# The first two FFN chunks prepared inside the attention, the weight units loaded earlier, and the experts chosen one softmax sooner

## The chip, the core and the metric

The kernel runs on one core of one Trainium2 chip. The metric is the device time of one execution in microseconds (us). The engines named below are TensorE (PE, its weight loads PEld), VectorE (DVE), ScalarE (ACT), GpSimd (POOL) and the SyncE queue (SP), which issues every DMA of this kernel.

## What is computed

The input has 4 images of 256 channels and 48 x 48 pixels. A block of attention by convolution is followed by a mixture of experts:

```
xn = layernorm over channels of x
k  = relu(conv7x7 with dilation 2 (xn, w1) + b1)          # 256 -> 128 channels
a  = softmax(relu(batchnorm(conv1x1(k, w2) + b2)))        # 49 maps
x  = x + sum over the 49 taps of shifted(xn) * a[tap]
t  = tokens of x;  n = layernorm(t)
g  = softmax(mean over tokens of n @ Wr + br)             # one row of 8 gates per image
g  = softmax(g * min(1, capacity / load))                 # capped gates
e  = the 2 largest of g; w = softmax of the two
y  = sum over the two experts of w * (gelu(n @ W1[e] + b1[e]) @ W2[e] + b2[e])
t  = t + layernorm(y + n) * gamma + beta
```

## The kernel before

Because of the dilation of 2, every 48 x 48 image is kept as four images of 24 x 24 pixels (by the parity of row and column). So there are 16 such images (`IMGS`), four to a batch `b` (`B` = 4). The numbers are float16 pairs: a high half and the low rest, so that each product takes three matmuls.

The program has two phases, each a block of its own; the second starts when every engine has ended the first.

**First phase (`mix_phase`), convolution.** For each batch the convolution runs over 14 points `k` (`NP`), with two halves of the channels (`c`) of 21 matmuls each (line 1316). A batch also does, between the points, what the batch before it still needs. In the last batch (b = 3) PE does after point k the logits of image k of batch 2 (`logits`, lines 1353 and 1357), and in the middle of point k the turning of the attention map of image k - 2 (line 1373). `logits` of one image waits until DVE has run `shift_logits` of the image before (line 1015 to 1020), since they share a PSUM bank. From point 9 on PE spreads the taps of the first 12 images (line 1404) in three PSUM banks; the fourth item waits until DVE has taken the low half of the first (`spread_low`, line 1129).

DVE runs its part of the same loop: for point k the layernorm's own work, `shift_logits` and `normalise` of image k - 1, the low half of the map, and `take_unit` (line 1098): the largest magnitude of one of 17 units of expert weights (8 of W1, one of all b1, 8 of W2), 512 KB each but for the small one. The dictionary `UNITS_SLOT` says how many units DVE takes at the end of each point. The units are loaded by SP (line 673) into three stages (`STAGES`) that lie in the dead tile `xs`; the load of unit u waits for `take_unit(u - 3)`. SP works strictly in the order of its program; before the change the first unit stands behind the layernorm numbers (lines 652 to 663), the attention maps (line 657, 2 x 459 KB) and the table `spread` (line 665, 684 KB).

**First phase, attention.** For each of the 16 images n, PE sums the taps (`attend`, line 1420, 39 matmuls in three groups, three PSUM banks), ACT adds the residual out of PSUM (`evict`, line 840), DVE takes the token statistics (`statistics`, lines 1063 to 1071) and sums of tokens (`accumulate`, line 1093), POOL raises to the power -0.5 (line 726), and SP stores the tokens and, for every fourth image, their statistics (`t_scratch`, `stat_scratch`, lines 642, 647, 649). The tables of the first 12 images (`EARLY`) lie in the first half of the tile `V`, `V[:, 0]`, which is dead once image 11 is attended. `load_back` brings the normalised images from DRAM.

**Second phase (`ffn_phase`).** The 9216 tokens are 24 chunks of 384, six to a batch. Of a chunk SP loads the tokens and their two statistics (lines 1666 and 1668), ACT normalises them (line 1837) and takes the high halves (line 1807), DVE takes the low halves (line 1916), and SP turns them by a transposing DMA into `xT` (line 1676). PE then runs layer 1 (line 2131, 48 matmuls) and layer 2 (line 2145, 72 matmuls). At the start, DVE, PE and ACT compute the gates in a chain of short instructions (lines 1882 to 1951). SP waits for the indices of the two experts, reads them, and loads their W1, b1, W2 and b2 (lines 1696 to 1709). ACT and DVE split W1 into halves (lines 1790 and 1959). For chunk 0 layer 1 waits for the turned tokens and for the high half of the first expert's W1.

## Time and profile before

| what | us |
|---|---|
| median of 3 runs | 980.85 |
| lowest and highest | 979.34, 983.98 |
| the profiled execution, its own time | 980.27 |
| its span in the trace | 978.5 |
| PE busy | 909.7 (93% of the span) |
| DVE busy | 699.5 (71%) |
| ACT busy | 528.8 (54%) |
| POOL busy | 141.8 (14%) |

The trace's clock starts at the span's start. The first phase ends at 576.2 us. The first phase's last batch of convolution begins near 345 us, its attention at 465 us. PE is the busiest engine; an interval in which PE is idle, or runs at the lower granted clock, is what to look for. "Granted clock" is the share of the full TensorE clock in a stretch; its two levels are 1.2 and 2.4 GHz (0.5 and 1.0). A row of a timeline gives start, duration, engine, line, operation, output and inputs, the number of instructions merged in it, and in square brackets the idle time ahead and what ended it.

### The profile page before, as it was taken

Reading aid. Unit: us, or ns where it says so; the run is one execution under the profiler, and the core shown is the slowest. Engines: PE = TensorE matmul, PEld = TensorE weight load, DVE = VectorE, ACT = ScalarE, POOL = GpSimd, SP = SyncE. Lnnn points to the kernel's source line nnn. Section 1 sums busy time; section 2 is a strip of 40 time slices with the busy share of each in tenths; the row PEclk is TensorE's granted clock in tenths of the full one; section 3 lists DMA queues with packets and bytes.
Section 4 is the critical chain, followed back from the end, with each engine's and each line's share of the span. In section 5 each row is a group of like instructions: output and inputs, shape, how many; then the busy total and the mean of one; then the engine's idle time right before and its main releaser. Section 6 shows DMA issues by size and latency. Waiting matters only on the chain. (4 is left out here: it accounts for less than half of the span.)

```text
span 978.5 us, 19546 instructions
## 1 busy us (share of the span) xinstructions
PE 909.7 (93%) x7659; PEld 755.1 (77%) x7659; DVE 699.5 (71%) x1824; ACT 528.8 (54%) x981; POOL 141.8 (14%) x164
## 2 busy tenths in 40 slices
PE   3787999999999969999999947999999999999997
PEld 2776888888888858888999934777777777777776
DVE  3797567477658619836579866878877887788777
ACT  4796343434444211133445438686867777687851
POOL 1100110000010200200113220111221212112122
PEclk9999999999999998989999968999999999999999
DMA  9721311132200144720558446354255335424211
GB/s 215 217 61 52 95 49 50 50 91 62 63 26 25 45 138 131 200 50 2 132 150 220 133 121 164 90 128 96 64 152 110 66 85 159 98 50 98 66 33 49
DMA packets 134826, 95.01 MB, mean 97 GB/s; under 512 B 63579, under 2 KB 129516, under 8 KB 134636
## 3 DMA queue, kind: packets, MB, share of 16 engines
q1 hardware_dynamic: 134734, 93.77, 37.5%
q8 instruction: 60, 0.98, 0.4%
q14 instruction: 32, 0.26, 0.1%
HBM read 54.91 MB, written 29.40 MB: 86 GB/s over the span
## 5 line engine op out<-in xcount | busy, mean ns | idle before, releaser
L1316 PE MATMUL pM<-V,U 128*128 128x264 f16 (+3 forms) x2352 | 294.6, 283 | 0.0
L1316 PEld LDWEIGHTS pM<-V,U 128*128 128x128 f16 x2352 | 230.5, 99 | 44.6
L1824 ACT ACTIVATE gf<-pH,b1c,sc 128x384 f32<-128x384 f32 x192 | 127.7, 669 | 83.8 <-issue 67.2
L2131 PE MATMUL pH<-xT,w1h 128*128 128x384 f16 x768 | 157.9, 329 | 5.8 <-DMA xT<-xs 3.4
L2145 PE MATMUL pY<-w2h,gh 128*128 128x256 f16 x576 | 157.0, 273 | 0.3 <-DVE w2l L1989 0.3
L2145 PE MATMUL pY<-w2h,gl 128*128 128x256 f16 x576 | 157.0, 273 | 0.0
L2145 PE MATMUL pY<-w2l,gh 128*128 128x256 f16 x576 | 157.0, 273 | 0.0
L1997 DVE SCALAR_TENSOR_TENSOR gl<-gf,sc,gh 128x384 f16<-128x384 f32 x192 | 112.1, 620 | 50.2 <-ACT gh L1815 50.2
L2131 PEld LDWEIGHTS pH<-xT,w1h 128*128 128x128 f16 x768 | 75.0, 99 | 55.6 <-ACT gf L1824 4.8
L1815 ACT ACTIVATE gh<-gf,sc 128x384 f16<-128x384 f32 x192 | 115.4, 616 | 0.0
L775 ACT CAST V<-pV 128x336 f16<-128x336 f32 x96 | 42.0, 437 | 133.3 <-PE pV L1287 133.3
L941 DVE TENSOR_TENSOR V<-pV,V 128x336 f16<-128x336 f32 x96 | 47.7, 501 | 71.3 <-ACT V L775 71.1
L2131 PE MATMUL pH<-xT,w1l 128*128 128x384 f16 x384 | 94.5, 328 | 0.0
L1757 POOL TENSOR_TENSOR tb<-tk,bet 128x768 f32<-128x768 f32 x24 | 43.6, 1817 | 302.1 <-DVE z L2009 278.7
L1287 PE MATMUL pV<-Td,xs 96*128 96x168 f16 x576 | 58.3, 237 | 5.7 <-DVE xs L1056 5.7
L2145 PEld LDWEIGHTS pY<-w2h,gh 128*128 128x128 f16 x576 | 56.4, 98 | 8.3 <-issue 0.7
L2145 PEld LDWEIGHTS pY<-w2l,gh 128*128 128x128 f16 x576 | 56.4, 98 | 7.6
L2145 PEld LDWEIGHTS pY<-w2h,gl 128*128 128x128 f16 x576 | 56.4, 98 | 6.5
L702 POOL TENSOR_TENSOR rstd<-ve,mhalf 96x6 f32<-96x6 f32 x16 | 21.2, 1322 | 258.3 <-DVE nmean L936 258.3
L2131 PEld LDWEIGHTS pH<-xT,w1l 128*128 128x128 f16 x384 | 37.8, 98 | 25.2 <-issue 0.7
L1287 PEld LDWEIGHTS pV<-Td,xs 96*128 96x128 f16 x576 | 46.7, 99 | 10.5 <-issue 6.4
L758 ACT ACTIVATE xa<-xa,shift,rstd 96x256 f32<-96x256 f32 x96 | 49.9, 594 | 7.6 <-POOL shift L704 7.5
(252 smaller groups left out, 1357.2 us busy)
## 6 DMA issues: line engine op xcount, KB each, us to landing
xa<-in_xt SPq DMA_DIRECT2D x16, 576.0 KB, 6.4
xs_scratch<-xs SPq DMA_DIRECT2D x16, 576.0 KB, 4.3
tk<-t_scratch SPq DMA_DIRECT2D x24, 384.0 KB, 3.8
out<-o SPq DMA_DIRECT2D x23, 384.0 KB, 2.9
xs<-in_ew SPq DMA_DIRECT2D x16, 512.0 KB, 4.3
U<-xs_scratch SPq DMA_DIRECT2D x16, 480.0 KB, 4.7
V<-in_w1g SPq DMA_DIRECT2D x6, 784.0 KB, 8.4
w1r<-in_ew SPq DMA_DIRECT2D x8, 512.0 KB, 4.3
```

Of the source, the lines that this page charges most:

```text
L702: nc.gpsimd.tensor_tensor(rstd[:, n % 2], ve[:, n % 2], mhalf[:, :], ALU.pow).then_inc(rstd_step, 1)
L758: last = nc.scalar.activation(xa[:, n % XBUFS, t, :], xa[:, n % XBUFS, t, :], ACT.Identity, bias=shift[:, n % 2, t:t + 1], scale=rstd[:, n ...
L775: nc.scalar.copy(v_out(0, m), v_in(m)).then_inc(vhi_ready, 1)
L941: tt(v_out(1, m), v_in(m), v_out(0, m), ALU.subtract).then_inc(vlo_ready, 1)
L1287: last = nc.tensor.matmul(v_in(m)[:, :, r * TR * TILES:(r + 1) * TR * TILES], xs[:, n % 2, 2 * g + r, a, c * P:(c + 1) * P], Td[:, d, :], ...
L1316: return nc.tensor.matmul(out[:, :, first:end], U[:, k, hi_u, piece, :], V[:, b % 2, hi_v, k, c, :, first + TILES * d:end + TILES * d], st ...
L1757: nc.gpsimd.tensor_tensor(tb[:, s], tk[:, m % TBUFS], bet[:, None, :].broadcast_to([P, CT, C]), ALU.add).then_inc(bias_added, 1)
L1815: nc.scalar.activation(gh[:, s, j, :], gf[:, (JB * m + j) % GBUFS, :], ACT.Copy, scale=scale_of(G_UP)).then_inc(gh_ready, 1)
L1824: nc.scalar.activation(gf[:, (JB * m + j) % GBUFS, :], pH[:, (JB * m + j) % HBUFS, 0:CN], ACT.Gelu, bias=b1c[:, j // FB, j % FB:j % FB + 1 ...
L1997: stt(gl[:, sl, j, :], gf[:, (JB * m + j) % GBUFS, :], scale_of(G_UP), gh[:, sl, j, :], ALU.mult, ALU.subtract).then_inc(g_step, 1)
L2131: last = nc.tensor.matmul(pH[:, (JB * m + j) % HBUFS, 0:CN], w[:, k, c, f * P:(f + 1) * P], xT[:, s, x, c, :], start=(i == 0), stop=(i == ...
L2145: last = nc.tensor.matmul(pY[:, t, 0:C], g[:, s, j, t * P:(t + 1) * P], w[:, j // FB, j % FB, :], start=(i == 0), stop=(i == len(terms) - 1))
```

## The change

Four things are changed.

1. The tile `V` and the buffers of the FFN's tokens (`tk`, `tnk`, `xs`, `xs2`, `xT`, in a new class `Tokens`) share one place: the latter are views of `V`. Those that chunks 0 and 1 need lie in `V[:, 0]`.
2. In the attention, SP loads chunks 0 and 1 after image 11 (`CHUNKS_AT`); ACT normalises and splits them after `evict(12)` and `evict(13)`; DVE takes the low halves at the end of its work for images 13 and 14; SP turns them after it has stored images 13 and 14. The same steps are gone from the start of the second phase.
3. The loads of the first three weight units stand ahead of the layernorm numbers, the maps and `spread`. `take_unit` is spread differently over the points: none at k = 0, one at k = 1, two at k = 2 to 6, three at k = 7 and 8 (before: one at k = 0 and two at each of k = 1 to 8).
4. The experts' indices are found from the capped gates ahead of the second softmax, which keeps their order. `MAX` and `MAX_INDEX` run there; `MAX` runs once more after it. SP waits for step 11 in place of 16.

```diff
-STAGES, UNITS_SLOT = 3, {0: 1, 1: 2, 2: 2, 3: 2, 4: 2, 5: 2, 6: 2, 7: 2, 8: 2}
+STAGES, UNITS_SLOT = 3, {1: 1, 2: 2, 3: 2, 4: 2, 5: 2, 6: 2, 7: 3, 8: 3}
...
+            sp.wait_ge(v_turned, V_TURNS * IMGS)
+            for s in range(2):
+                sp.wait_ge(xs_stored[s], 16 * IMGS // 2)
+            load_units(range(STAGES))
             sp.wait_ge(ln_taken, 2)
...
             sp.dma_start(G[:, :, :], spread_d).then_inc(g_loaded, 16)
-            for s in range(2):
-                sp.wait_ge(xs_stored[s], 16 * IMGS // 2)
-            sp.wait_ge(v_turned, V_TURNS * IMGS)
-            for u in range(UNITS):
...
+            load_units(range(STAGES, UNITS))
...
                 if n in STATS_AT:
                     store_stats(STATS_AT[n])
+                if n == CHUNKS_AT:
+                    sp.wait_ge(o_ready, T_SUMS * EARLY)
+                    sp.wait_ge(stats_stored[0], 32)
+                    for m in range(EARLY_CHUNKS):
+                        sp.wait_ge(t_stored[m], 32)
+                    for m in range(EARLY_CHUNKS):
+                        tokens.load(sp, 0, m)
+                if n - CHUNKS_AT - 2 in range(EARLY_CHUNKS):
+                    tokens.turn(sp, 0, n - CHUNKS_AT - 2)
...
+                if n - CHUNKS_AT - 1 in range(EARLY_CHUNKS):
+                    tokens.normalise(act, 0, n - CHUNKS_AT - 1)
+                    tokens.take_high(act, 0, n - CHUNKS_AT - 1)
...
+                if n - CHUNKS_AT - 2 in range(EARLY_CHUNKS):
+                    tokens.take_low(dve, 0, n - CHUNKS_AT - 2)
...
-            for m in range(2):
-                load_chunk(0, m)
-            sp.wait_ge(r_step, 16)
+            load_chunk(0, EARLY_CHUNKS)
+            sp.wait_ge(r_step, IDX_STEP)
             load_experts(0)
...
             do(tt(r[:, 6, :], r[:, 5, :], r[:, 4, :], ALU.mult))
+            do(nc.vector.max(r[:, 0, :], r[:, 6, :]))
+            do(nc.vector.max_index(idx[:, :], r[:, 0, :], r[:, 6, :]))
+            s.at(IDX_STEP)
             softmax_shift(r[:, 6, :], r[:, 2, :], 2)
             dve.wait_ge(r_exp, 2)
             softmax_divide(r[:, 3, :], r[:, 7, :], 3)
             do(nc.vector.max(r[:, 0, :], r[:, 7, :]))
-            do(nc.vector.max_index(idx[:, :], r[:, 0, :], r[:, 7, :]))
```

DVE in the last batch of the convolution, before, from point 0 (the copy of the layernorm numbers) into point 1; `largest` is a unit's largest magnitude, `mx` and `E` belong to `shift_logits` and `normalise`:

```order
L1110 TENSOR_SCALAR work<-pV 96x96 x2
L1098 TENSOR_REDUCE largest<-xs 128x1
L1015 TENSOR_REDUCE mx<-pL 96x6
L1017 TENSOR_SCALAR mx<-mx 96x6
L1020 SCALAR_TENSOR_TENSOR E<-pL,mx 96x294
```

The same place after:

```order
L1127 TENSOR_SCALAR work<-pV 96x96 x2
L1032 TENSOR_REDUCE mx<-pL 96x6
L1034 TENSOR_SCALAR mx<-mx 96x6
L1037 SCALAR_TENSOR_TENSOR E<-pL,mx 96x294
L1048 RECIPROCAL mx<-sizes 96x6
```

The first unit no longer stands ahead of the first `shift_logits`; it comes after that image's `normalise`. Further on, DVE from point 8 to the first items of the spreading, before:

```order
L1000 SCALAR_TENSOR_TENSOR work<-work 128x96x3 x4
L1098 TENSOR_REDUCE largest<-xs 128x1 x2
L1129 TENSOR_TENSOR U<-pV,U 120x48x8 x2
L1129 TENSOR_TENSOR U<-pL,U 120x48x8
```

and after:

```order
L1017 SCALAR_TENSOR_TENSOR work<-work 128x96x3 x4
L1115 TENSOR_REDUCE largest<-xs 128x1 x3
L1146 TENSOR_TENSOR U<-pV,U 120x48x8 x2
L1146 TENSOR_TENSOR U<-pL,U 120x48x8
```

Three units in place of two now stand ahead of the first low half of the spreading. ACT at the end of the attention, after (before, the four lines with `V<-V` are not there); `xs<-pM` and `V<-pM` are the evictions of images 12 to 15:

```order
L854 ACTIVATE xs<-pM,work 120x256 x4
L854 ACTIVATE xs<-pM,work 96x256
L1617 ACTIVATE V<-V 128x256 x3
L1627 ACTIVATE V<-V 128x384 x2
L854 ACTIVATE xs<-pM,work 120x256 x4
L854 ACTIVATE xs<-pM,work 96x256
L1617 ACTIVATE V<-V 128x256 x3
L1627 ACTIVATE V<-V 128x384 x2
L854 ACTIVATE V<-pM,work 120x256 x4
```

Normalising and splitting a chunk (3 + 2 instructions) now stand between the evictions of images 12, 13 and 14.

## Rows read from the trace of the kernel before

**Rows 1.** Chain that ended last: start, us, what (first, some, last)

```profile
577.25 4.13 DMA xs<-stat_scratch
...
585.04 4.63 DMA xT<-xs
589.72 5.31 PE pH L2131 x18
...
610.51 8.02 PE pY L2145 x72
...
955.96 7.87 PE pY L2145 x72
```

**Rows 2.** A stretch: busy us of PE, PEld, DVE, ACT, POOL; granted clock, DMA share, GB/s

```profile
367.30:373.30 6.00, 5.98 (x35) 4.83 (x36) 4.92 (x12) 1.00 (x3) 0.00 (x0) 0.58 0.49 155
```

**Rows 3.** Timeline of PE in the last batch's points 1 to 3

```profile
367.32 0.45 PE L1353 MATMUL pL<-bias_rows,bias_ones 128*96 128x294 bf16 x1 [8.62 <-DVE E L1020]
...
369.42 4.02 PE L1316 MATMUL pM<-V,U 128*128 128x288 f16 x21
...
377.29 2.58 PE L1316 MATMUL pM<-V,U 128*128 128x288 f16 x21
```

**Rows 4.** Timeline of DVE: first unit, units of point 7, first spread item

```profile
364.89 1.22 DVE L1098 TENSOR_REDUCE largest<-xs 128x1 f32<-128x1024 f32 x1 [13.99 <-DMA xs<-in_ew]
...
404.84 2.34 DVE L1098 TENSOR_REDUCE largest<-xs 128x1 f32<-128x1024 f32 x2
...
413.53 1.24 DVE L1129 TENSOR_TENSOR U<-pV,U 120x384 f16<-120x384 f32 x2 [0.60 <-ACT U L852]
```

**Rows 5.** Timeline of SP's queue: last map stores, first units

```profile
334.06 6.26 SPq L596 DMA_DIRECT2D attn_scratch<-work  x2
...
354.89 24.01 SPq L673 DMA_DIRECT2D xs<-in_ew  x8
```

**Rows 6.** Timeline of PE: fourth item of the spreading, a slow half point

```profile
414.17 0.86 PE L1404 MATMUL pV<-xa,U 113*128 113x48 f16 x8
...
420.01 4.26 PE L1316 MATMUL pM<-V,U 128*128 128x288 f16 x21
```

**Rows 7.** Timelines of SP, ACT and DVE at the end of the attention

```profile
549.21 0.48 SPq L649 DMA_DIRECT2D stat_scratch<-U  x1
...
552.24 1.47 ACT L840 ACTIVATE xs<-pM,work 120x256 f32<-120x256 f32 x3 [0.87 <-PE pM L1420]
554.61 1.02 ACT L840 ACTIVATE xs<-pM,work 120x256 f32<-120x256 f32 x2 [0.91 <-DVE U L1067]
...
566.93 1.32 DVE L1063 BATCH_NORM_STATS2 U<-V 120x6 f32<-120x256 f32 x3 [0.68 <-ACT V L840]
```

**Rows 8.** Timelines of DVE, ACT and SP at the start of the FFN

```profile
579.55 0.15 DVE L1882 TENSOR_REDUCE rc<-r 4x1 f32<-4x8 f32 x1
...
580.92 0.16 DVE L1933 MAX8 r<-r 4x8 f32<-4x8 f32 x1
...
581.41 1.58 ACT L1837 ACTIVATE tnk<-tk,xs 128x256 f32<-128x256 f32 x3 [1.21 <-DMA xs<-stat_scratch]
582.92 0.97 SPq L1699 DMA_DIRECT2D w1r<-in_ew  x2
583.02 0.94 ACT L1807 ACTIVATE xs<-tnk 128x384 f16<-128x384 f32 x2
583.99 1.03 DVE L1916 SCALAR_TENSOR_TENSOR xs<-tnk,xs 128x384 f16<-128x384 f32 x2 [0.90 <-ACT xs L1807]
...
586.94 2.37 ACT L1790 ACTIVATE w1h<-w1r,sc 128x1024 f16<-128x1024 f32 x2
```

**Rows 9.** Around the FFN's start: loads of w1r, of statistics, the transposes (ns)

```profile
DMA to landing us min/median/max: 3.7/4.2/4.6
...
DMA to landing us min/median/max: 2.7/3.3/5.8
...
L1676 SPq DMA_TRANSPOSE xT<-xs x3: 1441/2641/4125, 585.0 to 605.6; - x3
```

More of the change, by code:

```diff
@@ L206 @@
 ADDED, BY_PE = 1, IMGS - 2
+CHUNKS_AT = EARLY - 1
 def window(d, h, w):
@@ L231, in mix_phase @@
 def mix_phase(nc, xt, w1g, b1, w2, b2, bn_gamma, bn_beta, bn_mean, bn_var, ident_d, spread_d, data_d, tap_d, xs_d, attn_d, ln_d, t_d, stat_d,
-              mean, ident, const_loads, experts, largest, wsum):
+              mean, ident, const_loads, experts, largest, wsum, V, tokens):
     PIECES = CC * KS
@@ L649, in store_stats, with load_units @@
                 sp.dma_start(rows[:, (NB - 1) * TB:], sT[(NB - 1) * 2 * BI:, b % 2, 0:TL]).then_inc(stats_stored[b % 2], 16)
+            def load_units(units):
+                for u in units:
+                    if u >= STAGES:
+                        sp.wait_ge(unit_taken, u - STAGES + 1)
+                    src, dst = unit(u)
+                    sp.dma_start(dst, src).then_inc(unit_loaded[u % STAGES], 16)
+            sp.wait_ge(v_turned, V_TURNS * IMGS)
+            for s in range(2):
+                sp.wait_ge(xs_stored[s], 16 * IMGS // 2)
+            load_units(range(STAGES))
             sp.wait_ge(ln_taken, 2)
@@ L1556 @@
 XSLOTS, XAHEAD = 4, 3
+EARLY_CHUNKS = 2
 X_SCALE = 32.0
@@ L1568, in ffn_phase @@
+def ffn_phase(nc, mean, wsum, consts, tokens, ew1, eb1, ew2, eb2, gamma, beta, out):
     ident, wrs, brs = consts
@@ L1633, in ffn_phase @@
         bias_step = sem("bias_step")
-        tk_loaded = [sem(f"tk_loaded{s}") for s in range(TBUFS)]
-        tn_made = sem("tn_made")
-        x_turned = [sem(f"x_turned{s}") for s in range(2)]
-        xh_ready = sem("xh_ready")
-        xl_ready = sem("xl_ready")
         h_ready = sem("h_ready")
@@ L1664, in load_chunk @@
                     sp.wait_ge(bias_added, n - TBUFS + 1)
[L1665 to L1677 removed]
+                tokens.load(sp, b, m)
+            def turn_x(b, m):
+                after(sp, h_ready, JB * (CHUNKS * b + m - XSLOTS + 1))
+                tokens.turn(sp, b, m)
             def store_chunk(b, m):
@@ L1801, in take_x @@
             def take_x(b, m):
-                n, s = CHUNKS * b + m, m % 2
-                if n >= 2:
-                    act.wait_ge(x_turned[s], 16 * (n // 2))
-                act.wait_ge(tn_made, 2 * (n + 1))
-                for c in range(CC):
-                    last = nc.scalar.activation(xs2[:, s, 0, c], tnk[:, m % NBUFS, :, c * P:(c + 1) * P], ACT.Copy, scale=X_SCALE)
-                last.then_inc(xh_ready, 1)
+                tokens.take_high(act, b, m)
             def gelus(b, m):
@@ L1835, in normalise @@
                     act.wait_ge(z_step, (n - NBUFS) * Z_ALL + 4)
-                for t in range(CT):
-                    last = nc.scalar.activation(tnk[:, m % NBUFS, t, :], tk[:, m % TBUFS, t, :], ACT.Identity,
-                                                bias=xs[:, m % TBUFS, 1, t:t + 1], scale=xs[:, m % TBUFS, 0, t:t + 1])
-                last.then_inc(tn_made, 2)
+                tokens.normalise(act, b, m)
             for k in range(2):
-                act.wait_ge(r_step, (2, 11)[k])
+                act.wait_ge(r_step, (2, IDX_STEP + 2)[k])
                 nc.scalar.activation(r[:, 2 * k + 1, :], r[:, 2 * k, :], ACT.Exp).then_inc(r_exp, 1)
-            normalise(0, 0)
-            take_x(0, 0)
-            act.wait_ge(r_step, 17)
+            act.wait_ge(r_step, R_STEPS - 4)
             nc.scalar.activation(rc[:, 5:6], rc[:, 4:5], ACT.Exp).then_inc(r_exp, 1)
             nc.scalar.activation(rc[:, 7:8], rc[:, 4:5], ACT.Gelu)
-            normalise(0, 1)
             split_w1(0)
-            take_x(0, 1)
             act.wait_ge(bias_step, 1)
@@ L1912, in take_x @@
             def take_x(b, m):
-                n, sl = CHUNKS * b + m, m % 2
-                dve.wait_ge(xh_ready, n + 1)
-                for c in range(CC):
-                    last = stt(xs2[:, sl, 1, c], tnk[:, m % NBUFS, :, c * P:(c + 1) * P], X_SCALE, xs2[:, sl, 0, c],
-                               ALU.mult, ALU.subtract)
-                last.then_inc(xl_ready, 1)
+                tokens.take_low(dve, b, m)
             dve.wait_ge(r_pe, 1)
```

94 lines of the change are left out of this document (60 added, 34 removed).

## The prediction

> **What bounds the kernel now.** I read the chain of waits first. From 610.5 us on it is nothing but PE: layer 1 and layer 2 of one chunk after the other until 963.8, in pieces of 7.8 and 7.9 us [rows 1]. The change touches no matmul of that stretch, so its 353 us move as a block and the whole question is when it starts. Ahead of it stand two DMAs of chunk 0: the statistics, then the transpose that ends 0.05 us before PE's first matmul [rows 1]. Before 576 us PE bounds as well, and there I looked for its idle time. The largest idle interval behind the start-up is 8.62 us ahead of 367.32, ended by DVE's `shift_logits` [rows 3]. DVE itself had stood 13.99 us on the DMA of the first weight unit [rows 4]: the unit was taken at 364.89, though SP had issued it at 354.89, behind the maps, the layernorm numbers and the table [rows 5]. None of the numbers behind that unit were needed by anybody then. DVE's queue is in order, so `shift_logits` of image 8 stood behind it, and the logits of image 9 behind that.
>
> **Part 1: the first units, early.** SP stores the last maps until 340.3 [rows 5] and then issues nothing for some 10 us, until the layernorm numbers are turned in the last batch's first point. The three loads now go out in that gap. A load of a unit lands in 3.7 to 4.6 us by the nearest rows, W1 of the experts with the same size [rows 9]; three of them are there before 350, and DVE wants the first only behind `normalise`, near 357. The stall of 8.62 us goes. With it goes its after-effect: the granted clock was 0.58 in the 6.0 us behind the stall [rows 2], where a half point took 4.02 us and later ones 2.58 [rows 3]. At full clock those 6.0 us are 3.5, so 2.4 us more are saved: **-11.0 us**. What is late next? DVE's pace over the points 1 to 5 is that of before (some 6.6 us a point, PE 6.4 with its logits and turnings), and it starts 11.5 us sooner while PE starts 11.0 sooner, so no new wait arises there; in my walk through the points the turning of image 11's map has the least room, about 1 us. Bounds: 8.6 us if the slow clock falls into another stretch, 11.1 if all of it goes.
>
> **Part 2: three units at points 7 and 8.** A unit takes DVE 1.17 us (two in 2.34) [rows 4]. Before, DVE was done with the last unit at 412.93 and took the first low half of the spreading at 413.53, after ACT's high half [rows 4]; PE's fourth item ran at 414.17 [rows 6], just as the bank came free. So DVE had 0.6 us of room in this place. One more unit in each of two points is 2.3 us. DVE arrives 0.5 us earlier with respect to PE (11.5 against 11.0), but loses some 0.5 to 1 us at point 6, because a unit's load waits for the take of the unit three before it, and those come closer together. The last take then ends 2.3 to 2.9 us later against PE, the first low half begins 1.7 to 2.3 us later, and PE waits that long ahead of the fourth item: **+2.0 us**. Bounds: 0.6, if the loads come fast and DVE's lead holds, to 3.5, if the slow clock of 420.01 (4.26 us for a half point [rows 6]) comes earlier or once more and costs its 1.7 us.
>
> **Part 3: the chunks in the attention.** SP reaches the new loads when it has issued the statistics of images 4 to 7, at 549.69 [rows 7]; its other new waits are long met. Chunk 0 is three DMAs, tokens and two rows of statistics; at 0.5 us each, as the one at 549.21, the last goes out near 550.7. In the FFN the same load landed 4.13 us after its issue [rows 1]; all loads of statistics landed in 2.7 to 5.8 us [rows 9]. With 4.13, chunk 0 is there at 554.8. ACT is done with image 12 at 553.71 [rows 7], waits 1.1 us, and needs 1.58 + 0.94 = 2.52 us [rows 8] for the chunk. Behind it in ACT's queue stands the eviction of image 13, which began at 554.61 [rows 7] and now begins at 557.35: 2.7 us late. PE waits for that eviction, since the first group of image 14 needs its bank: I expect PE to stand there 1 to 1.5 us. DVE waits for it as well, and has two low halves of 1.03 us each more [rows 8]. At the end of the phase every step waits for the one before (statistics of image 15, POOL's power, sum, turning, store), and DVE had only 0.68 us of idle time ahead of the last part of those statistics [rows 7]. So the end of the phase is at least 2.06 - 0.68 = 1.4 us late by DVE alone; by ACT's delay it is 2.7. I take **+2.6 us**, nearer to ACT's, because there DVE waits for ACT. Bounds: 1.4, and 4.3 if the load lands in 5.8 us.
>
> SP's queue has two transposes more, each waiting for DVE's low half. The second ends its issue between 571 and 573.5; the last statistics are ready for SP near 575. The row for the transposes holds SP for 1.4 to 4.1 us each [rows 9], and I used the 4.1. The Trainium skill (Advanced Engine Details and Errata, X-Bar Transpose) says that on trn2 "transpose DMAs are as fast as regular DMAs". By it SP would be free some 3.5 us sooner; the row speaks against it, at least for the issue. By either the sum is the same, and only the room ahead of the last store differs.
>
> **Part 4: the start of the FFN.** Counted from the phase's start. Before, the indices came behind a second softmax; `MAX` ran at 580.92 and can now run at 579.55, where that softmax began [rows 8]: 1.37 us. SP then needs 1.6 us to read them, as before, and issues W1. The first W1 landed 3.7 us after 582.92 [rows 8, 9], at 586.6; ACT, busy with chunk 1, began the high half at 586.94 [rows 8] and had the first at 588.1. PE could have begun then but waited for the transpose until 589.72 [rows 1]. Now chunk 0 is turned, ACT has nothing else, and PE begins 1.6 (the transpose) + 1.37 (the indices) + 0.3 (ACT) = 3.3 us sooner; the low half of W1 may cost 0.1 of it. **-3.2 us**. From PE's start on to layer 2 of chunk 0 the chain has the same members as before (Gelus, chunk 2, splitting of W2). Bounds: 2.3 if the W1 lands in 4.6 us, 3.4. The later `MAX` (0.16) and moving of W2's loads ahead of everything else cost nothing: nobody waits for them there.
>
> **The sum** against the profiled execution's own 980.27 (span 978.5 and 1.8 around it): -11.0 + 2.0 + 2.6 - 3.2 = -9.6, so 970.7. That execution lies 0.6 below the median, hence **971.3 us**.
>
> **Rivals.**
> *The clock pays part back.* Between 416 and 444 us the granted clock falls for a half point at a time without PE being idle [rows 6]; a wait of 2 us in this same place could lower it once or twice more, at 1.7 us each. For it: it fell behind the long stall [rows 2]. Against: no fall follows PE's two waits of 1.2 us, near 465 and 548. With DVE at its worst (+1.5): 971.3 + 1.5 + 2.5 = 975.3.
> *The chunks come late.* The load lands at 5.8 us or later, or behind the token stores: +1.7 to +3.4, 973 to 974.7.
> *The units are late all the same.* If something holds SP ahead of the three loads, DVE stands at point 1 instead of point 0: the take would end at 366.1, `shift_logits` of image 9 at 367.2, and PE would want it at 365.1. The stall shrinks only to 2.1 us, some of the slow clock stays: 971.3 + 2.1 + 1.2 = 974.6.
> *It falls better.* One slow half point disappears with the new alignment and part 2 costs 0.6: 971.3 - 1.7 - 1.4 = 968.2.
> *Slower than before.* ACT's queue is in order, and the wait for chunk 0's load stands ahead of the eviction of image 13. Each us of wait beyond 1.1 delays the end by one. The rest of the change saves 9.6, so it decides from a landing 13.7 us after its issue (4.1 + 9.6); at 16 us the kernel would take 983. Against it: the slowest such load took 5.8 [rows 9].
>
> **How the numbers follow.** Forecast (969 to 973) 0.52; the clock 0.12; late chunks 0.12; late units 0.06; better 0.10; slower 0.03; two of the first three together, around 977, 0.05. The range, 968.0 to 975.5, leaves out the last two and the far ends of the others. About 0.5% is what a measurement of this kernel can tell from no change: 975.9 and 985.8. Faster 0.90, same 0.07, slower 0.03.
>
> **What would show it.** In the changed profile: PE's wait of 8.6 us for DVE's `E` gone and no granted clock of 0.58 behind it; the first unit taken near 357 without DMA wait; PE idle some 2 us ahead of the fourth spread item near 403, ended by DVE's low half; ACT idle about 1 us on the chunk's statistics, PE idle 1 to 1.5 us within image 14; the second phase starting 11.0 - 2.0 - 2.6 = 6.4 us sooner, at 569.8; PE's first layer 1 matmul 10.3 us behind that (before 13.5), released by ACT's `w1h`. I am wrong if a wait of PE over 2 us appears between 360 and 400, if the clock's falls differ by more than 4 us in sum, or if the chunk loads land after 558.

## The result: 974.0 us, 0.992 of the kernel before

| | before | after |
|---|---|---|
| median, beside each other on one chip (7 runs each) | 979.34 us | 974.01 us |
| lowest and highest | 978.03, 983.98 | 967.95, 976.42 |
| ratio, 95% interval | 1 | 0.9922, 0.9899 to 0.9945 |
| same pair on another chip (17 and 8 runs) | 982.00 us | 973.33 us, 0.9913, 0.9876 to 0.9949 |
| profiled execution, own time; span | 980.27; 978.5 | 967.95; 966.2 |
| granted clock, mean of that execution | 0.966 | 0.972 |

The change is worth 0.8%, about 7.6 us. The ratio goes with the means of the seven runs (980.3 and 972.6); the medians alone lie only 5.3 us apart. The profiled execution of the changed kernel is the fastest of its seven; the two profiles are therefore 12.3 us apart, more than the medians. For this reason I compare stretches between fixed events, and not the two spans.

**PE's first stretch.** PE's timeline at points 0 and 1 of the last batch, after. Columns as in [rows 3].

```profile
351.46 0.29 PE L1372 MATMUL pL<-bias_rows,bias_ones 128*96 128x294 bf16 x1
...
352.56 5.00 PE L1335 MATMUL pM<-V,U 128*128 128x288 f16 x42
357.40 0.29 PE L1372 MATMUL pL<-bias_rows,bias_ones 128*96 128x294 bf16 x1
```

The second logits begin 5.9 us behind the first, with no bracket: the 8.62 us of [rows 3] are gone. SP's and DVE's timelines say why; the three loads stand alone in the gap between the last maps and the layernorm numbers, and the first unit is taken without a wait (in [rows 4] 13.99 us for the DMA):

```profile
339.32 1.45 SPq L657 DMA_DIRECT2D xs<-in_ew  x3
349.79 0.33 SPq L664 DMA_DIRECT2D ln_scratch<-work  x1
```

```profile
356.25 1.21 DVE L1115 TENSOR_REDUCE largest<-xs 128x1 f32<-128x1024 f32 x1
```

**The fourth item of the spreading**, PE's and DVE's timelines, after:

```profile
403.42 1.22 DVE L1115 TENSOR_REDUCE largest<-xs 128x1 f32<-128x1024 f32 x1 [1.50 <-DMA xs<-in_ew]
404.55 0.55 DVE L1146 TENSOR_TENSOR U<-pV,U 120x384 f16<-120x384 f32 x1
```

```profile
405.16 0.85 PE L1423 MATMUL pV<-xa,U 113*128 113x48 f16 x8 [3.16 <-DVE U L1146]
405.83 4.90 PE L1335 MATMUL pM<-V,U 128*128 128x288 f16 x21
```

In [rows 6] PE reached this item as the bank came free. Now it waits 3.16 us for the low half, which stands behind the seventeenth unit, and 1.50 us of that is DVE's own wait for this unit's load. The half point behind it took 4.90 us in place of 2.60, at the low clock.

**The end of the attention and the start of the FFN.** ACT's timeline behind image 12, after:

```profile
543.60 1.58 ACT L1617 ACTIVATE V<-V 128x256 f32<-128x256 f32 x3
545.21 0.94 ACT L1627 ACTIVATE V<-V 128x384 f16<-128x384 f32 x2
546.05 2.35 ACT L854 ACTIVATE xs<-pM,work 120x256 f32<-120x256 f32 x5
```

The normalising of chunk 0 has no bracket: in this execution ACT did not wait for the load, and PE's timeline shows no wait between the images 12 and 14 either, where 1 to 1.5 us were forecast. The eviction of image 13 starts 9.33 us behind the start of image 12 at 536.72, against 6.23 before [rows 7 and the 548.38 of the trace]; 1.7 us of this is a low clock at image 12, since ACT is done with that image 6.99 us behind its start, before 5.33. SP spent much less on the turning than the longest row of [rows 9]:

```profile
552.28 1.57 SPq L1641 DMA_TRANSPOSE V<-V  x1
...
557.76 1.46 SPq L1641 DMA_TRANSPOSE V<-V  x1
```

The chain of waits of the changed kernel, at the start of the FFN:

```profile
572.60 3.72 DMA w1r<-in_ew
576.34 1.16 ACT w1h L1848
577.63 4.06 PE pH L2169 x12
...
598.24 8.02 PE pY L2183 x72
```

The transpose of [rows 1] is no member any more; the indices' W1 and its high half are. The second phase starts at 567.32 (forecast 569.8), PE's first layer 1 at 577.63, 10.3 us behind it. From layer 2 of chunk 0 to the end of the span it is 367.96 us, before 367.99: this block moved whole.

### The profile page after: what moved, and what is told of

Its sections match the earlier page's. It is cut to its first block and busy times, and to the rows that moved or that the text cites. A ratio compares the mean times of both kernels' runs of the same rounds, so it can differ in the third digit from the quotient of the medians.

```text
span 966.2 us, 19549 instructions
## 1 busy us (share of the span) xinstructions
PE 905.5 (94%) x7659; PEld 752.6 (78%) x7659; DVE 698.6 (72%) x1825; ACT 528.8 (55%) x981; POOL 143.4 (15%) x164
## 5 line engine op out<-in xcount | busy, mean ns | idle before, releaser
L1335 PE MATMUL pM<-V,U 128*128 128x264 f16 (+3 forms) x2352 | 291.3, 281 | 0.0
L2169 PE MATMUL pH<-V,w1h 128*128 128x384 f16 x768 | 157.7, 328 | 4.4 <-ACT gf L1876 2.4
L2169 PEld LDWEIGHTS pH<-V,w1h 128*128 128x128 f16 x768 | 74.9, 98 | 54.1 <-ACT gf L1876 4.8
L1867 ACT ACTIVATE gh<-gf,sc 128x384 f16<-128x384 f32 x192 | 115.5, 616 | 0.0
L2169 PE MATMUL pH<-V,w1l 128*128 128x384 f16 x384 | 94.5, 328 | 0.0
L1815 POOL TENSOR_TENSOR tb<-V,bet 128x768 f32<-128x768 f32 x24 | 43.5, 1813 | 298.8 <-DVE z L2048 281.9
L2169 PEld LDWEIGHTS pH<-V,w1l 128*128 128x128 f16 x384 | 37.6, 98 | 25.5 <-DVE w1l L1998 0.6
L1306 PEld LDWEIGHTS pV<-Td,xs 96*128 96x128 f16 x576 | 46.6, 99 | 11.1 <-issue 7.1
```

The costliest lines, as they stand in the source:

```text
L1306: last = nc.tensor.matmul(v_in(m)[:, :, r * TR * TILES:(r + 1) * TR * TILES], xs[:, n % 2, 2 * g + r, a, c * P:(c + 1) * P], Td[:, d, :], ...
L1335: return nc.tensor.matmul(out[:, :, first:end], U[:, k, hi_u, piece, :], V[:, b % 2, hi_v, k, c, :, first + TILES * d:end + TILES * d], st ...
L1815: nc.gpsimd.tensor_tensor(tb[:, s], tk[:, m % TBUFS], bet[:, None, :].broadcast_to([P, CT, C]), ALU.add).then_inc(bias_added, 1)
L1867: nc.scalar.activation(gh[:, s, j, :], gf[:, (JB * m + j) % GBUFS, :], ACT.Copy, scale=scale_of(G_UP)).then_inc(gh_ready, 1)
L2169: last = nc.tensor.matmul(pH[:, (JB * m + j) % HBUFS, 0:CN], w[:, k, c, f * P:(f + 1) * P], xT[:, s, x, c, :], start=(i == 0), stop=(i == ...
```

## One table for all traces

Six events occur in every kernel of this study: T, the first matmul of the logits of image 8 (before 352.60); A, the first of the attention (465.12); I, the first of image 12 (548.38); F, the start of the second phase (576.20); L, the first matmul of layer 1 (589.72); Y, the first of layer 2 (610.51). All are starts in PE's timeline (F is 0.36 us ahead of its first matmul there). T to A is split into PE's idle and busy time, by a window of just this stretch. The windows of before, after and e11, columns as in [rows 2]:

```profile
352.60:465.12 112.52, 102.69 (x893) 88.73 (x891) 70.72 (x145) 24.42 (x50) 7.59 (x6) 0.91 0.39 112
```

```profile
351.46:455.12 103.66, 99.30 (x893) 86.63 (x891) 70.31 (x145) 24.53 (x50) 7.59 (x6) 0.95 0.39 106
```

```profile
352.84:451.00 98.16, 96.95 (x893) 85.61 (x891) 70.48 (x145) 24.53 (x50) 7.59 (x6) 0.98 0.40 112
```

It is the same 893 matmuls each time. The kernels of the experiments go by the first part of their labels; their edits are below.

| kernel | T to A | idle | busy (clock) | A to I | I to F | F to L | L to Y |
|---|---|---|---|---|---|---|---|
| before | 112.52 | 9.83 | 102.69 (0.91) | 83.26 | 27.82 | 13.52 | 20.79 |
| after | 103.66 | 4.36 | 99.30 (0.95) | 81.60 | 30.60 | 10.31 | 20.61 |
| e7 (after again) | 103.36 | 3.39 | 99.97 (0.95) | 84.92 | 30.62 | 10.38 | 20.65 |
| e8 | 101.52 | 1.50 | 100.02 (0.95) | 81.60 | 29.48 | 13.70 | 21.08 |
| e9 | 112.16 | 7.79 | 104.37 (0.91) | 81.60 | 29.48 | 13.59 | 20.92 |
| e5 | 104.35 | 2.52 | 101.83 (0.93) | 83.25 | 30.01 | 10.23 | 22.51 |
| e1 | 112.62 | 9.98 | 102.64 (0.91) | 83.25 | 29.93 | 10.27 | 22.49 |
| e3 | 102.88 | 4.19 | 98.69 (0.97) | 86.00 | 27.82 | 12.98 | 21.11 |
| e6 | 105.02 | 3.37 | 101.65 (0.94) | 81.60 | 29.48 | 10.20 | 21.08 |
| e10 | 102.25 | 2.08 | 100.17 (0.95) | 83.26 | 27.80 | 10.54 | 20.63 |
| e4 | 102.76 | 3.97 | 98.79 (0.97) | 86.49 | 30.62 | 12.02 | 20.11 |
| e11 | 98.16 | 1.21 | 96.95 (0.98) | 81.59 | 30.60 | 10.31 | 20.61 |
| e12 | 103.93 | 3.98 | 99.95 (0.95) | 84.92 | 38.56 | 10.30 | 20.22 |
| e13 | 98.51 | 1.31 | 97.20 (0.98) | 86.48 | 29.47 | 10.50 | 22.44 |

Busy times differ by the granted clock alone. In two more columns it shows without any edit near it. A to I holds the same matmuls in all fourteen traces, and yet it takes 81.6, 83.3, 84.9 or 86.0 to 86.5 us. I to F takes 27.8 or 29.5 us where nothing was put into it. The last experiment shows the rows.

A part of this is only where a slow stretch falls. PE's timelines at image 12, before and after:

```profile
548.38 12.99 PE L1420 MATMUL pM<-U,V 120*120 120x256 f16 x117 [1.16 <-DVE V L1129]
```

```profile
536.72 14.92 PE L1439 MATMUL pM<-U,V 120*120 120x256 f16 x117 [1.16 <-DVE V L1146]
```

Before, a slow stretch ends ahead of I (granted clock 0.50 from 541 to 543); after, it stands behind I (0.60 from 536.72 to 539.90). So A to I and I to F must be read together. A to F is 111.1 us in before, e6, e8, e9 and e10, 113.8 in e3 and 116.0 in e13, all without work on the chunks between the images; with this work it is 112.2 in after and e11, 113.2 and 113.3 in e1 and e5, 115.5 in e7, 117.1 in e4, and 123.5 in e12.

## Experiments

Each ratio is to the kernel before on the same chip. e8, e9, e5 and e1 share a chip (before 978.82 us), e3, e7, e6 and e10 another (982.00), e4, e11 and e12 a third (979.54); e13 ran on a fourth (979.33).

### The loads early, and nothing else (e8)

```diff
+            sp.wait_ge(v_turned, V_TURNS * IMGS)
+            for s in range(2):
+                sp.wait_ge(xs_stored[s], 16 * IMGS // 2)
+            load_units(range(STAGES))
             sp.wait_ge(ln_taken, 2)
...
-            for u in range(UNITS):
...
+            load_units(range(STAGES, UNITS))
```

This is the kernel before with these lines; the takes stay at {0: 1, 1: 2, ... 8: 2}.

> The kernel before with one edit: the loads of the first three weight units stand ahead of the layernorm numbers, maps and table; the takes stay where they were (one at point 0). Theory A (the unit's late landing holds DVE, and DVE holds the logits of image 9): DVE takes the first unit near 350 without a DMA wait, PE's wait of 8.6 us and the slow clock behind it are gone, 11 us less, and since points 7 and 8 keep two takes the fourth spread item does not wait: about 969.5, ratio 0.989. Theory B (the take itself must stand behind shift_logits to matter): DVE is still held at point 0 and the time stays within 3 us of before. Theory C (the DMA engines are the limit, the maps and the table only come later): the stall is gone, but PE waits for the turned-back layernorm numbers or the first spread item instead, several us.

970.06 us, ratio 0.9899 (0.9873 to 0.9924). T to A is 11.0 us shorter than before. DVE takes the first unit without a wait:

```profile
350.38 1.21 DVE L1102 TENSOR_REDUCE largest<-xs 128x1 f32<-128x1024 f32 x1
```

From T to A PE waits only 0.30 us behind another engine, and 1.2 us just ahead of A as in the other traces, so Theory B falls, and Theory C too. One instruction stream moved on one queue carries the whole gain. The full change has 0.9922; the difference lies within the two intervals.

### The takes moved, and nothing else (e9)

```diff
-STAGES, UNITS_SLOT = 3, {0: 1, 1: 2, 2: 2, 3: 2, 4: 2, 5: 2, 6: 2, 7: 2, 8: 2}
+STAGES, UNITS_SLOT = 3, {1: 1, 2: 2, 3: 2, 4: 2, 5: 2, 6: 2, 7: 3, 8: 3}
```

> The kernel before with one edit: the takes are spread as in the change (none at point 0, one at point 1, three at points 7 and 8); the loads stay where they were. Theory A: the first unit still lands near 365, but now it is waited for behind shift_logits of image 8, so that it holds only shift_logits of image 9; PE stands about 2 us ahead of the logits of image 10 in place of 8.6, little slow clock; then the fourth spread item waits 2 to 3 us, with slow clock behind it up to 2.3 us more. In sum 4 to 7 us less than before, ratio 0.993 to 0.996. Theory B (the order of the takes is the whole gain): as the changed kernel without its FFN part, 7 us less or more.

979.95 us, ratio 1.0018 (0.9996 to 1.004): none of the expected gain. The stall of 8.62 us is gone here too, but three others stand in its place. PE's timeline of this kernel, the idle rows between 360 and 412:

```profile
365.64 0.30 PE L1353 MATMUL pL<-bias_rows,bias_ones 128*96 128x294 bf16 x1 [1.42 <-DVE E L1020]
...
384.79 0.92 PE L1373 MATMUL pA<-ident,E 96*66 96x96 f32 x6 [2.80 <-DVE xa L1051]
...
410.85 0.85 PE L1404 MATMUL pV<-xa,U 113*128 113x48 f16 x8 [2.34 <-DVE U L1129]
```

DVE still waited 6.64 us for the first unit, one point later. The three waits are 6.6 us. Behind the second and the third (a half point of 4.64 us from 411.52 on) the clock is low, as it had been behind the one long stall: idle time 2.0 us less than before, busy time 1.7 us more, 0.4 us gained. The window behind the second wait:

```profile
384.80:389.60 4.80, 4.80 (x29) 3.58 (x30) 4.71 (x7) 0.66 (x2) 0.00 (x0) 0.64 0.34 81
```

The expectation had priced the first and the third of these waits; the second, of 2.80 us behind DVE's `xa`, and the low clock behind it were not in it.

### The old takes in the changed kernel (e5)

The line of e9 the other way round, on the changed kernel.

> The changed kernel, but the takes as before the change (one at point 0, two at points 1 to 8); the loads of the first three units stay early. Theory A: DVE takes the first unit at once, no stall there; DVE is done at point 8 in time, PE's wait of 3.2 us ahead of the fourth spread item falls to under 1 us and the half point behind it (4.90 us in the changed kernel) runs at 2.6: 3 to 5.5 us less than the changed kernel, about 969. Theory C (the clock falls in this stretch whatever PE waits for): the wait goes, the slow half point stays: 3 us less at most.

969.13 us, ratio 0.9875 (0.9841 to 0.991), below the changed kernel's 0.9922. The wait ahead of the fourth item is gone, but the half point behind it is slow all the same, which is what Theory C said. PE's timeline:

```profile
402.98 0.86 PE L1423 MATMUL pV<-xa,U 113*128 113x48 f16 x8
403.66 4.26 PE L1335 MATMUL pM<-V,U 128*128 128x288 f16 x21
```

T to A is no shorter in this trace (104.35 against 103.66): PE's idle time is 1.8 us less, but the clock is lower (0.93 against 0.95) and gives 2.5 us of busy time back. The idle time that is left is a wait of 1.32 us at 381.10 for DVE, which had waited 1.88 us for a unit's load. The ratios, measured on two chips, are 0.0047 apart, with 0.0042 for their joint interval: that the changed takes cost is likely by them and no more; e11 shows it and says how.

### The units as before in the changed kernel (e1)

Both edits of e8 and e9 undone on the changed kernel, so that only the chunks and the indices are left of the change.

> The changed kernel with the units as before the change (loads behind the table, takes from point 0 on); chunks in the attention and early indices stay. Theory A (most of the change's gain is in the units): the stall of 8.6 us and the slow clock are back, the wait at the fourth spread item is gone: within 2 us of the kernel before, 977 to 980, since the two other parts give only 0.6 us together by my sum. Rival: the chunks and the indices carry the gain, and this one stays near 974.

978.32 us, ratio 0.9975 (0.9955 to 0.9996). Its I to F and F to L against before: +2.1 and -3.25, together -1.1 us. Here the picture that I drew of the attention's end appears nearly to the number, since the clock is full there. ACT's and PE's timelines of this kernel:

```profile
554.27 1.58 ACT L1616 ACTIVATE V<-V 128x256 f32<-128x256 f32 x3 [0.88 <-DMA V<-stat_scratch]
...
556.73 2.35 ACT L853 ACTIVATE xs<-pM,work 120x256 f32<-120x256 f32 x5
```

```profile
557.87 4.44 PE L1438 MATMUL pM<-U,V 120*120 120x256 f16 x39 [1.07 <-ACT xs L853]
```

ACT waits 0.88 us for the load (forecast 1.1), the eviction of image 13 comes 8.67 us behind image 12 instead of 6.23 (2.4 late, forecast 2.7), PE waits 1.07 us within the last images (forecast 1 to 1.5).

### The chunks prepared in the FFN again (e3)

On the changed kernel, the four blocks of the diff with `CHUNKS_AT` are gone, and at the start of the second phase stand again:

```diff
+            for m in range(EARLY_CHUNKS):
+                load_chunk(0, m)
             sp.wait_ge(r_step, IDX_STEP)
             load_experts(0)
...
+            normalise(0, 0)
+            take_x(0, 0)
```

> The changed kernel with chunks 0 and 1 loaded, normalised, split and turned at the start of the second phase, as before; the early units, the moved takes and the earlier indices stay. Theory A (the sum of parts 3 and 4 as I took it): the second phase starts 2.6 us sooner with respect to the start of image 12, PE's first matmul of layer 1 stands 13.5 us behind that start instead of 10.3, released by the transpose again; together 0.6 us later than the changed kernel, 0.9995 to 1.001 of it. Theory B (by the run with only the units undone, which gave 0.9975 of the kernel before, and by the run with the old takes against the one with the early loads alone, 0.9875 against 0.9899): the chunks and the indices are worth 2.4 us, so this kernel is 2.4 us slower than the changed one, about 0.9945 of the kernel before.

973.82 us, ratio 0.9919, beside 973.33 and 0.9913 for the changed kernel on the same chip (e7). The intervals are 0.6% wide, so Theory B's 2.4 us are not excluded by the times; the trace is of Theory A: I to F 27.82 (2.8 less than e7, 2.15 less than e1 and e5, which had the full clock), F to L 12.98 (2.6 more). From A to F it is 1.7 us less than e7. So moving the chunks is worth little by itself: 2.6 us gained at the FFN's start, 1.1 to 2.2 paid in the attention (A to F of after, and of e1 and e5, against 111.1). The early indices give only 0.5 us of F to L here, since PE waits for the transpose again.

### The changed kernel again (e7)

> The changed kernel itself once more, beside the next three on the same chip, so that they can be held against it and not only against the kernel before. Theory A (its ratio of 0.992 is a property of the kernel): 0.990 to 0.994, about 971.2 us if the kernel before is at 978.8. Theory B (its profiled run of 967.95 was the usual one and the median of 974 a matter of that chip): about 0.989. Its profile should again show PE waiting about 3.2 us ahead of the fourth item of the spreading, and the first matmul of layer 1 10.3 us behind the start of the second phase; the half points at the low clock may stand elsewhere.

973.33 us, ratio 0.9913 (0.9876 to 0.9949), as Theory A has it; the interval does not exclude the 0.989 of Theory B. PE waits 2.18 us ahead of the fourth item, less than the 3.2 expected, and F to L is 10.38.

### The indices late again (e4)

```diff
-            sp.wait_ge(r_step, IDX_STEP)
+            sp.wait_ge(r_step, IDX_STEP + 7)
```

> The changed kernel, with SP waiting for the end of the second softmax before it reads the indices, as before the change (DVE's instructions stay in the new order). Theory A (with the chunk turned ahead of time, the chain index, W1, high half of W1 is what PE waits for): W1's loads go out 1.4 us later, and so does PE's first matmul of layer 1: 11.7 us behind the start of the second phase in place of 10.3, released by the high half of W1. Total 1.4 us more than the changed kernel (0.14%, less than the interval will be wide; the trace decides). Rival B (another member is late next, for instance the Gelu or layer 2's weights): the first matmul is later, but layer 2 of chunk 0 is not.

973.85 us, ratio 0.9941 (0.992 to 0.9962). F to L is 12.02 us, 1.7 more than the changed kernel. ACT's timeline names the wait (in the changed kernel it is 1.85 us):

```profile
582.72 1.15 ACT L1848 ACTIVATE w1h<-w1r,sc 128x1024 f16<-128x1024 f32 x1 [3.56 <-DMA w1r<-in_ew]
```

F to Y is 32.13 against 30.92, so 1.2 us of it reach layer 2; the clock rose a little sooner behind L (20.11 against 20.61). Rival B, by which none of it would, falls. Two parts of the change belong together: the early indices are worth 1.7 us where the chunk is turned ahead of time and 0.5 where it is not.

### The chunks behind the last image (e6)

```diff
-                if n - CHUNKS_AT - 1 in range(EARLY_CHUNKS):
-                    tokens.normalise(act, 0, n - CHUNKS_AT - 1)
-                    tokens.take_high(act, 0, n - CHUNKS_AT - 1)
+            for m in range(EARLY_CHUNKS):
+                tokens.normalise(act, 0, m)
+                tokens.take_high(act, 0, m)
```

and the same for DVE's low halves and SP's turning (of chunk 1 at the start of the second phase, where the load of chunk 2 now stands behind those of the experts).

> The changed kernel with the work on chunks 0 and 1 behind that of the last image instead of between images 12 and 14: ACT normalises and splits them after the eviction of image 15, DVE takes the low halves behind the last statistics, SP turns chunk 0 behind the last statistics' store and chunk 1 at the start of the second phase. The loads stay where they are. Theory A (part 3's cost is the queue of ACT and DVE ahead of the last images): the second phase starts 2 to 2.8 us sooner with respect to image 12, the first matmul of layer 1 stays 10.3 us behind it (up to 11.5 if the transpose of chunk 0 now ends last), total 1.5 to 2.8 us less than the changed kernel, a ratio to it of 0.997 to 0.9985. Theory B (the end of the attention is bound by the chain of the last statistics, and ACT had room): no difference, within 0.5 us.

970.17 us, ratio 0.9899 (0.9849 to 0.9948), 0.9968 of e7 by medians. The interval is too wide to call it from the time. In the trace I to F is 29.48, what it is in e8 and e9, where nothing was put there, and 1.1 less than in the changed kernel; F to L stays at 10.20. That is less than the 2 to 2.8 us of Theory A, and not nothing: A to F is 111.1, as in the kernel before. So the two chunks are free at this place in the trace, and the cost of part 3 was their place in ACT's and DVE's queues.

### Both at once: late split and old takes (e10)

> The kernel of the late split with the takes of the units as they were before the change (one at point 0, two at each of points 1 to 8), the three loads still early. If both losses are real and add up: 0.9875 of the kernel before from the takes kept, less another 1.5 to 2.8 us, that is 0.985 to 0.986, about 964 to 965.5 us. If the late split brings nothing: 0.9875, 966.6. If the clock takes back what is gained (the run with the old takes had a low clock in layer 1 of chunk 1 where the changed kernel had none): 0.988 to 0.990.

966.49 us, ratio 0.9847 (0.9803 to 0.989). A to F is 111.1 and F to L 10.54: both gains together, with no wait at the fourth item. e6 on the same chip differs from it in the takes alone; the means are 4.8 us apart, +- 4.2.

### One take less at point 7 (e11)

```diff
-STAGES, UNITS_SLOT = 3, {1: 1, 2: 2, 3: 2, 4: 2, 5: 2, 6: 2, 7: 3, 8: 3}
+STAGES, UNITS_SLOT = 3, {1: 2, 2: 2, 3: 2, 4: 2, 5: 2, 6: 2, 7: 2, 8: 3}
```

> The changed kernel with two units taken at point 1 and two at point 7, in place of one and three; three stay at point 8 and none at point 0. Every take from point 2 on comes one unit sooner. Theory A (PE's wait ahead of the fourth item of the spreading is DVE's queue of takes, which had no room): one take of 1.17 us less stands ahead of the first low half, and the DMA wait of 0.6 to 1.5 us of the last unit shrinks, so PE's wait there falls from 2.2 to 3.2 us to 0.5 to 1.5 us; in exchange one take more stands in front of the shift of image 10's logits, which may show as a wait of PE up to 1 us near 365 to 381. Total 0.5 to 2 us less than the changed kernel. Theory B (the loads' pace sets it, each load waiting for the take three before): the wait stays at 2 to 3 us, since the last unit is loaded no sooner.

965.26 us, ratio 0.9855 (0.9823 to 0.9888) against 0.9922 for the changed kernel: 6.6 +- 3.9 us less by the ratios, more than either theory allowed. DVE's and PE's timelines of this kernel, from point 8 to the first items:

```profile
399.35 3.51 DVE L1115 TENSOR_REDUCE largest<-xs 128x1 f32<-128x1024 f32 x3
402.78 1.03 DVE L1146 TENSOR_TENSOR U<-pV,U 120x384 f16<-120x384 f32 x2
```

```profile
403.38 0.85 PE L1423 MATMUL pV<-xa,U 113*128 113x48 f16 x8
404.05 2.60 PE L1335 MATMUL pM<-V,U 128*128 128x288 f16 x21
...
409.21 2.60 PE L1335 MATMUL pM<-V,U 128*128 128x288 f16 x21
...
415.00 2.60 PE L1335 MATMUL pM<-V,U 128*128 128x288 f16 x21
...
420.98 4.01 PE L1335 MATMUL pM<-V,U 128*128 128x288 f16 x21
```

The three takes at point 8 are one block without a DMA wait, the first low half begins 44.0 us behind the second logits instead of 47.2, and PE's wait of 3.16 us is 0. One unit moved, worth 1.17 us of work, took away 3.2 us of wait, since the loads' wait of 1.50 us went with it: the load of a unit waits for the take three before it, and the take had come sooner. Idle time from T to A is 1.21 us against 4.36, and the clock is 0.98 against 0.95, since one half point is slow in place of two: 96.95 us busy against 99.30. Together 5.5 us, of which I had foreseen less than half. Theory A is right in its sign, Theory B falls.

The half point behind the fourth item shows what the wait takes with it. In all seven traces in which PE waits there, for 2.16 to 3.16 us (after, e3, e4, e6, e7, e9, e12), it is slow, 3.81 to 4.90 us; of the seven without the wait it takes 2.60 us in six and 4.26 in e5. Without the wait the low clock is thus rarer in this place, but not excluded.

### The chunks loaded one image later (e12)

```diff
-                if n == CHUNKS_AT:
+                if n == CHUNKS_AT + 1:
```

> The changed kernel with the loads of chunks 0 and 1 one image later in SP's queue, behind the stores of image 12; ACT, DVE and the turning stay as they are. This makes the load late on purpose, the mechanism of the rival in which the kernel gets slower. In the changed kernel the load went out at 538.2 and the store of image 12 at 543.7; here the load goes out near 545.5 and lands 4.1 us later, at 549.7, while ACT reaches it at 543.6. Theory A (ACT's queue is in order and there is no room behind it): ACT waits 6 us there, the eviction of image 13 is 6 us late, and the second phase starts 4.5 to 6 us later, so the kernel takes 4.5 to 6 us more, 0.997 to 0.998 of the kernel before. Rival B (the end of the attention has room on ACT, since the POOL and DVE steps bound it): less than 2 us more.

978.72 us, ratio 0.9982 (0.9958 to 1.0006): nearly the whole gain of the change is lost. ACT's and PE's timelines:

```profile
553.96 1.58 ACT L1617 ACTIVATE V<-V 128x256 f32<-128x256 f32 x3 [6.83 <-DMA V<-stat_scratch]
```

```profile
557.56 6.31 PE L1439 MATMUL pM<-U,V 120*120 120x256 f16 x39 [7.02 <-ACT xs L854]
```

ACT waits 6.83 us for the load (chunk 0's DMAs go out from 548.18 on, 10 us later than in the changed kernel), PE 7.02 us for the eviction behind it, and the 39 matmuls of the image then run in 6.31 us, where at full clock they take 4.4. I to F is 38.56, 8.0 us more than in the changed kernel. So the rival in which the kernel becomes slower had its mechanism right, and its price of one us for each us of wait nearly: 6.83 us of wait cost 8.0, more than the 4.5 to 6 expected here, since the clock is low behind PE's pause. The gain is used up at a wait of about 7 us; the changed kernel had 0 to 1.

### Both repairs of the changed kernel (e13)

e6 with the takes of e11.

> The changed kernel with both of its measured losses mended: two takes at point 1 and two at point 7 (which alone gave 0.9855 of the kernel before), and the chunks normalised, split and turned behind the last image (which let the second phase start 1.1 us sooner with respect to image 12 beside a low clock and 2.1 us sooner without). If they add up: 0.9855 less 1.1 to 2.1 us, that is 0.9834 to 0.9844 of the kernel before, with no wait of PE ahead of the fourth item and 27.8 to 29.5 us from the start of image 12 to the second phase. If the granted clock takes it back: 0.985 to 0.987, with the same waits but two or more slow half points where the run with one take less had one.

968.14 us, ratio 0.9877 (0.985 to 0.9903): the gains did not add up, and against e11 (0.9855, on another chip) the intervals overlap. The waits are as expected (none at the fourth item, T to A 98.51, I to F 29.47). That the clock takes it back holds, but not where it was expected: from T to A one half point is slow, as in e11, and the loss lies behind A. The windows from A to I, columns as in [rows 2], of e13, then of e11, then of the kernel before:

```profile
450.12:536.60 86.48, 85.32 (x902) 84.41 (x902) 62.24 (x236) 41.55 (x87) 18.86 (x24) 0.90 0.59 158
```

```profile
451.00:532.59 81.59, 80.43 (x902) 79.87 (x903) 61.69 (x236) 41.59 (x87) 18.83 (x24) 0.96 0.62 167
```

```profile
465.12:548.38 83.26, 82.11 (x902) 81.42 (x902) 62.38 (x236) 41.59 (x87) 18.86 (x24) 0.94 0.61 164
```

The same 902 matmuls, PE idle for 1.2 us in each, and 4.9 us of difference; what differs is the granted clock, 0.90, 0.96, 0.94. The second place is within layer 1 of chunk 0. PE pauses there for 2.35 to 2.45 us for a Gelu in every kernel of this study. In eleven of the fourteen traces the matmuls behind the pause run at the full clock; in e1, e5 and e13 they do not, and L to Y is 1.4 to 1.9 us longer than in before, after, e6 or e8. PE's timelines, of the changed kernel and of e1:

```profile
592.89 0.82 PE L2169 MATMUL pH<-V,w1h 128*128 128x384 f16 x4 [2.36 <-ACT gf L1876]
```

```profile
604.28 1.46 PE L2168 MATMUL pH<-V,w1h 128*128 128x384 f16 x4 [2.36 <-ACT gf L1875]
```

The best kernels measured are thus e10 (0.9847) and e11 (0.9855), both better than the changed one; their intervals overlap, and which is better stays open. e13 has the fewest waits and, in its trace, a lower clock.

## Why the prediction was right, point by point

The forecast was 971.3 us in 968.0 to 975.5; the median is 974.0, inside, 2.7 above. Held against the stretches:

**Part 1, -11.0.** e8 has it alone: T to A -11.0, of it 8.3 us of idle time (forecast 8.6) and 2.7 us of low clock (forecast 2.4). The steps hold as well, in the changed kernel: loads in the gap, first take at 356.25 (forecast near 357) without a wait, no stall, no clock of 0.58 behind it.

**Part 2, +2.0.** PE's idle time from T to A is 3.4 to 4.4 us in the six traces with the early loads and these takes, on the mean 3.9, against 1.5 to 2.5 in e8, e10 and e5 with the old ones: +1.9, with one row behind it of 2.2 to 3.2 us ahead of the fourth item (the old takes have smaller waits of their own near 381, which I had not seen). The step that was short is the units' loads. I gave them 0.5 to 1 us at point 6, and there DVE's waits of 1.00 and 1.67 us stand beside 1.32, 0.29 and 0.17 before, 0.9 more. The wait of 1.50 us for the seventeenth unit, right ahead of the low half, was in no term. Parts 1 and 2 together were to be -9.0; T to A in those six traces is on the mean 103.6 us against 112.5 and 112.6, so -8.9 to -9.0. Against the three traces with the old takes (102.7) it is 0.9 us longer, against e11 5.4.

**Part 3, +2.6.** This term was too large: +2.15 where the clock is full at image 12 (e1, e5), +1.1 where it is low (after, e7, against e8, e9), the latter below my bounds of 1.4 to 4.3. Where the clock is low at image 12, PE itself is late and the load has landed before ACT wants it: that cover I did not see (no run tests it by itself). With image 12 at the full clock, in e1, the members are near the forecast. The transposes hold SP for 1.57 and 1.46 us, so the row of 4.1 that I used was the wrong one of the three. I had weighed against it the Trainium skill (Advanced Engine Details and Errata, X-Bar Transpose), by which transposing DMAs are as fast as others on this chip; the trace agrees on the way to the landing, 3.8 us at the median for the two turnings beside 3.5 and 4.2 for the large stores of the images around them, and not on the issue, 1.5 us against 0.4 to 0.7 for one of these stores. Neither value entered the sum.

**Part 4, -3.2.** F to L 10.31 against 13.52: -3.2. Its members: with the chunk's part undone 12.98 (e3), with the indices' part undone 12.02 (e4). The forecast gave the indices 1.37 of it; measured 1.7.

**The sum.** -8.86, +1.12, -3.39 from T to A, A to F and F to Y in the profiled pair make -11.1, forecast -9.6; the profiles differ by 12.3, since everything up to T was 1.1 us shorter. With I to F alone (+2.78) in place of A to F the sum would be -9.5 and look like the forecast; that is luck, since 1.66 us of it is the slow stretch that stood ahead of I before and behind it after. The medians differ by 5.3 us, and the ratio gives 7.6 +- 2.3. That the median of 974.0 lies in the range is in part luck too: the stretches gave 1.5 us more than forecast, and the ratio 2.0 us less. What lies between the profiles and the ratio goes with the clock: over the 143 executions for which it is on record, each against the mean of its own group, 0.001 of mean granted clock goes with 0.84 us (correlation -0.93), and the seven executions of the changed kernel have 0.962 to 0.972. In which stretches it differs is seen only in the profiled ones. I allowed for falls of the clock near the wait only.

**The rivals.** "The clock pays part back" is half true: the half point behind the wait took 4.90 us (3.83 in e7), but in place of the three slow half points of before, 420.01 among them [rows 6], there are two in this trace; the other five traces with this wait and early loads have two to four. What I held against this rival, that no low clock follows PE's wait of 1.2 us at image 12, is true of the trace before and not of the one after (the rows at 548.38 and 536.72). "The chunks come late" did not happen, and e12 shows what it would have cost. "The units are late all the same" did not happen; e9 shows a version of it. "Slower" was real as a mechanism and needed 7 us.

**Room.** I asked of part 2 what it costs and not whether it is needed. e8, e5 and e10 show that once the loads are early, the old takes need no change: none of them has a wait at the fourth item, and none of their ratios (0.9899, 0.9875, 0.9847) is above the 0.9922 of the change, though only that of e10 is well clear of it. e11 shows that one unit moved back does as well.

## What to carry to other kernels

When a stall is a load that waits behind work nobody needs, move the load and then look whether the rest of the repair still has a purpose: here the moved work behind it cost 3 us at a place with 0.6 us of room. Price a step put into a queue by who stands behind it there; the same two chunks cost 1 to 2 us between the last images and nothing behind them. On a kernel that PE fills, compare several traces over stretches between fixed events before a difference of 2 us is believed: one profile against one profile gave -12.3 where the ratio gave -7.6. Then look whether a slow stretch has only passed from one side of an event to the other, as here at image 12.

## What the runs showed of the hardware

- The granted clock falls to half for some 3 us at a time in stretches in which PE has no idle time, and at which point it falls differs between kernels that do the same there: the same 902 matmuls took 81.6 us in e11 and 86.5 in e13, whose attentions start 0.9 us apart.
- Behind PE's wait of 2.2 to 3.2 us ahead of the fourth item the next half point was slow in seven of seven traces; without the wait in one of seven.
- Behind one and the same pause of 2.35 to 2.45 us, entered at the full clock, PE came back at the full clock in eleven kernels and at half in three.
- A transposing DMA of one chunk held the issuing queue for 1.5 and 1.6 us in the attention, and for up to 4.1 us at the start of the FFN before [rows 9].
